# Window attention and a convolution on one core: split keys copied between partitions in place of a round trip through device memory

## Chip, core and metric

The program runs on one core of one Trainium2 chip. The metric is the time of one execution on the device in microseconds (us); of several runs the median is taken. The engines are TensorE (PE, matmuls; PEld is its weight loads), VectorE (DVE), ScalarE (ACT), GpSimd (POOL) and SyncE (SP), which here does nothing but issue transfers (DMAs) and wait.

## What is computed

Two residual steps on x of shape (2, 128, 128, 128), each behind a group norm with 32 groups. The first is attention in 8 by 8 windows with 16 heads of 8 channels, the second a 3 by 3 convolution. Cut to its core:

```
x = x + attention(group_norm(x))
x = x + conv3x3(group_norm(x)) + bias

attention(v):   g = clip((v * ac_w + ac_b) * v, 0, 6)
                q, k, v = qkv_w @ g, per window of 64 pixels and head of 8 channels
                o = softmax(q k^T / sqrt(8)) v
                return proj_w @ o + proj_b
```

## The kernel before, in words

For each of the 2 images there is an attention stage and then a convolution stage. The attention stage cuts the image into 32 units of 512 pixels (8 windows). It is a software pipeline written out by hand: each engine has a function `one` that is called once per iteration and issues its share of the work for units that lie up to 5 ahead and 3 behind. Order within an engine is the order of the code; between engines only semaphores order the work. `after(engine, s, unit)` waits until the event `s` of that unit has happened. Three buffers (`BUFS`) of each operand rotate.

The steps that the change and the prediction touch, for a unit d, with the lines of the kernel before:

- PE projects keys and queries into PSUM (`project`, L853 to L855). Each is split into a high half (fp16) and a low half (the rest, fp16), so that products keep their precision: ACT writes the high halves into the tile `qk` (keys L495, queries L503), DVE the low halves (queries L690, keys L692). `qk` has one buffer: parts 0 and 1 hold the low and high queries, 2 and 3 the high and low keys.
- The score matmuls want another layout: for a head the 8 channels times 3 halves (the "stack": high, low, high for keys; low, high, high for queries) must lie on 24 neighbouring partitions. [...]
- PE computes the scores of the unit twice: once plain (`scores`, L885) for the row maxima, which DVE takes (L654), and, an iteration later, transposed (`scores_t`, L899) with the maxima as two more rows of the stack, for ACT's exponentials (L448).
- The maxima of all heads are transposed by PE (L975), split by ACT (L499) and DVE (L686) into `m_pair`, and carried by SP into two rows of `q_bd` (`maxima`, L288, four transfers of 32 rows to one partition each).
- PE then multiplies with the values (`weigh`, L918, L926) and projects (L995).

SP goes through these transfers in a fixed order, one after the other: queries of a unit in, keys in, the maxima of the unit before it, the writes of the next unit, and so on. A wait at SP holds up all that stands behind it. ACT may overwrite the keys in `qk` (L495) once the write of the previous unit's keys has landed (`k_sent`), the queries (L503) once theirs has (`q_sent`).

The transposition L975 happens once per unit, so the time between two of them is the length of a unit.

Of the kernel before, what the change touches and what calls it, by code (L numbers as in the profile page):

```python
# [6 lines left out]
F16 = mybir.dt.float16  # L7
ALU = mybir.AluOpType
# [3 lines left out]
P = 128  # L12
# [10 lines left out]
UT = UW * WIN  # L23
# [3 lines left out]
HR, HG, HJ = 2, 4, 2  # L27
# [8 lines left out]
BUFS = 3  # L36
# [24 lines left out]
def build(nc, x, ac_w, ac_b, qkv_w, proj_w, proj_b, conv_w, conv_b, out):  # L61

    stackd = nc.dram_tensor("stack_scratch", [BUFS, 2, P, PARTS, UT], F16, kind="Internal").ap()

    ctx = ExitStack()
    with ctx:
# [73 lines left out]
        def sem(name, per=1):  # L140
            s = ctx.enter_context(nc.semaphore(name))
            names[name] = (s, per)
            return s
# [7 lines left out]
        v_out = sem("v_out", 4)  # L151
        q_sent = sem("q_sent", 32); k_sent = sem("k_sent", 32)
        q_in = sem("q_in", 64); k_in = sem("k_in", 32)
        s_done = sem("s_done", 4); max_done = sem("max_done", 4)
# [25 lines left out]
        def after(eng, s, unit, k=None):  # L180

            name = next(n for n, (h, _) in names.items() if h is s)
            per = names[name][1]
            eng.wait_ge(s, unit * per + (AHEAD * per + (per if k is None else k)))

        def pixels(u):

            return (u // ACROSS) * WS, (u % ACROSS) * UCOL

        block = ctx.enter_context(nc.Block())  # L190
# [52 lines left out]
        def _(sp):  # L243
# [13 lines left out]
            for b in range(BATCH):  # L257
                def write(which, d, md, lo, sent):
                    after(sp, lo, d)
                    to = stackd[md, which]  # L260
                    sp.dma_start(to[:, 0:2, :], qk[:, 2 * which:2 * which + 2, :]).then_inc(sent, 16)
                    sp.dma_start(to[:, 2, :], qk[:, 1 + which, :]).then_inc(sent, 16)

                def queries_in(d, md):
                    after(sp, q_sent, d)
                    after(sp, st_done, d - BUFS)
                    after(sp, q_in, d - 1)
                    q_rows = stackd[md, 0].rearrange("(r g j d) s t -> r j (d s) g t", r=HR, g=HG, j=HJ)
                    for r in range(HR):
                        for j in range(HJ):  # L270
                            at = 64 * r + HROWS * j
                            sp.dma_start(q_bd[at:at + HROWS, md, r, :, j, :], q_rows[r, j]).then_inc(q_in, 16)

                def keys_in(d, md):
                    after(sp, k_sent, d)
                    after(sp, st_done, d - BUFS)
                    after(sp, k_in, d - 1)
                    k_rows = stackd[md, 1].rearrange("(r g a) s t -> r (a s) g t", r=HR, g=HG)
                    for r in range(HR):
                        sp.dma_start(k_pl[64 * r:64 * r + ROWS, md, :, :], k_rows[r]).then_inc(k_in, 16)  # L280

# [9 lines left out]
                def one(i, m, live):  # L291
                    n = i + b * UNITS
                    if live(3):
                        queries_in(n + 3, (m + 3) % BUFS)
                        keys_in(n + 3, (m + 3) % BUFS)
                    if live(2):
                        maxima(n + 2, (m + 2) % BUFS)
                    if live(4):
                        after(sp, q_in, n + 1)
                        write(0, n + 4, (m + 4) % BUFS, q_lo_done, q_sent)  # L300
                        after(sp, k_in, n + 1)
                        write(1, n + 4, (m + 4) % BUFS, k_lo_done, k_sent)
                iterations(b, one)
# [119 lines left out]
        def _(act):  # L423
# [11 lines left out]
            act.wait_ge(pe_step, 3)  # L435
            a.copy(w_hi[:, :, :], ps[:, 0, 0:3 * P].rearrange("p (t d) -> p t d", t=3)).then_inc(act_step, 1)
            act.wait_ge(pe_step, 4)
            a.copy(pw[:, :], ps[:, 1, 0:P]).then_inc(act_step, 1)
            for b in range(BATCH):
# [25 lines left out]
                def one(i, m, live):  # L465
# [26 lines left out]
                    if live(3):  # L492
                        after(act, k_done, n + 3)
                        after(act, k_sent, n + 2)
                        a.copy(qk[:, 2, :], ps[:, GB, :]).then_inc(k_hi_done, 1)  # L495
# [59 lines left out]
        def _(dve):  # L555
# [41 lines left out]
            def weak_weights():  # L597

                for j in range(MATS // 4):
                    dve.wait_ge(act_step, 3 + j)  # L600
                    v.tensor_tensor(c_lo[:, 4 * j:4 * j + 4, :], ps[:, 2 + j, :].rearrange("p (t d) -> p t d", d=P),
                                    c_hi[:, 4 * j:4 * j + 4, :], ALU.subtract).then_inc(weights_done, 1)

            flat = img[:, :, :].rearrange("p r c -> p (r c)")
            for i in range(UNITS):
                if i == 2:
                    dve.wait_ge(act_step, 1)
                    link(v.tensor_tensor(w_lo[:, :, :], ps[:, 0, 0:3 * P].rearrange("p (t d) -> p t d", d=P), w_hi[:, :, :], ALU.subtract))
                dve.wait_ge(x_in[i * LOADS // UNITS], 16)
                stats = v.bn_stats(st[:, i, :], flat[:, i * UT:(i + 1) * UT])  # L610
# [208 lines left out]
        def _(pe):  # L819
# [36 lines left out]

            pe.wait_ge(act_step, 2)
            norm_mean(0)
# [188 lines left out]
```

## Time and profile before

| | us |
|---|---|
| median of 3 runs | 1202.87 |
| lowest, highest | 1198.44, 1207.99 |
| profiled execution, its own time | 1207.08 |
| its span, first to last instruction | 1205.3 |
| PE busy | 1015.8 (84% of the span) |
| DVE busy | 983.1 (82%) |
| ACT busy | 791.3 (66%) |
| mean granted TensorE clock | 0.947 of full speed |

The profile shows one execution. The first attention stage lies at about 40 to 470 us, the first convolution at 470 to 640, the second attention stage at 640 to 1060 and the second convolution behind it. SP has no busy time on the page, since issuing a transfer is not counted; the timeline of SP shows it: each row there is the issue of one or more transfers with the time that SP spent on it, not the transfer itself. "Landing" is the time from the start of an issue until its semaphore says that the data has arrived. "issue" as a releaser means that the profile shows nothing that the engine waited for, though a semaphore of a transfer may stand behind it.

### The profile page before, as it was taken

What the parts mean: (1) busy time and instruction counts of PE and PEld (TensorE: products, weight loads), DVE (VectorE), ACT (ScalarE), POOL (GpSimd) and SP (SyncE); (2) the same over time, 40 slices, a digit from 0 to 9 for tenths busy, and PEclk for the clock granted to TensorE, in tenths of its full rate; (3) what the DMA queues carried; (4) which work ended last, traced back from release to release, by engine and by line L of the source; (5) the groups of instructions that cost most, each with busy time, mean ns of one, the idle gap of its engine ahead of it and who ended that gap; (6) DMA issues with size and microseconds to landing.
All of it is one profiled execution on the core that took longest, in us unless ns stands there. A gap on an engine that the chain in (4) does not pass through costs nothing.

```text
span 1205.3 us, 52690 instructions
## 1 busy us (share of the span) xinstructions
PE 1015.8 (84%) x23011; PEld 582.6 (48%) x23011; DVE 983.1 (82%) x1312; ACT 791.3 (66%) x1327; POOL 503.8 (42%) x469
## 2 busy tenths in 40 slices
PE   0388999999999985998853899999999999779996
PEld 0155565556555652433321555556655655334442
DVE  6786888889888754899986788888988976379996
ACT  1257787778778774655532688878887877556663
POOL 5214454445444433233343245545454544404335
PEclk9879999999999997999986899999999999879998
DMA  8234444444444420133343454444444444001112
GB/s 307 84 118 125 136 138 138 136 137 128 135 142 135 142 64 1 44 129 108 105 157 122 123 150 139 136 137 138 144 132 148 134 142 126 4 1 53 70 70 88
DMA packets 114917, 140.59 MB, mean 117 GB/s; under 512 B 25088, under 2 KB 91008, under 8 KB 113664
## 3 DMA queue, kind: packets, MB, share of 16 engines
q1 hardware_dynamic: 114688, 137.23, 36.3%
q8 instruction: 182, 2.98, 1.1%
q14 instruction: 47, 0.39, 0.1%
HBM read 67.96 MB, written 67.11 MB: 112 GB/s over the span
## 4 chain that ended last, share of the span: by engine, by line
PE 63%; DVE 18%; issue 8%; DMA 4%; ACT 3%; SPq 2%; POOL 2%; POOLq 0%; DVEq 0%; ACTq 0%
PE ps L918 11%; PE ps L899 11%; PE ps L926 9%; PE ps L885 8%; PE ps L995 6%; PE ps L853 5%; DVE work L760 5%; PE ps L854 5%; PE ps L855 5%; DVE work L756 4%; PE ps L872 4%; DVE st L610 1%; SPq L288 1%; DVE work L738 1%; DMA q_bd<-stack_scratch 1%
## 5 line engine op out<-in xcount | busy, mean ns | idle before, releaser
L654 DVE TENSOR_REDUCE m_all<-ps 128x16 f32<-128x1024 f32 x256 | 313.5, 1225 | 114.9 <-PE ps L885 114.3
L370 POOL TENSOR_SCALAR work<-work 128x256 f32<-128x256 f32 x128 | 108.6, 849 | 401.2 <-DVE work L647 352.4
L885 PEld LDWEIGHTS ps<-k_pl,q_bd 48*64 48x64 f16 x8192 | 90.4, 111 | 174.5 <-issue 126.9
L448 ACT ACTIVATE late_probs<-ps,ws 128x1024 f32<-128x1024 f32 x128 | 142.8, 1116 | 44.6 <-PE ps L899 42.8
L853 PE MATMUL ps<-work,c_hi 128*128 128x512 f16 x384 | 148.3, 386 | 27.7 <-DVE work L760 27.7
L899 PE MATMUL ps<-q_bd,k_pl 128*64 128x256 f16 x2048 | 163.8, 282 | 7.5 <-ACT work L448 4.0
L885 PE MATMUL ps<-k_pl,q_bd 48*64 48x64 f16 x8192 | 118.6, 198 | 57.3 <-issue 39.4
L536 ACT CAST work<-work 128x512 f16<-128x512 f32 (+1 forms) x128 | 79.0, 622 | 115.8 <-DVE work L756 107.9
L448 ACT ACTIVATE work<-ps,ws 128x1024 f32<-128x1024 f32 x128 | 141.7, 1107 | 13.1 <-PE ps L899 11.5
L854 PE MATMUL ps<-work,c_lo 128*128 128x512 f16 x384 | 148.0, 385 | 0.0
L855 PE MATMUL ps<-work,c_hi 128*128 128x512 f16 x384 | 147.4, 384 | 0.0
L380 POOL TENSOR_TENSOR g_both<-work,g_both 128x512 f16<-128x512 f32 x64 | 99.9, 1561 | 54.4 <-ACT g_both L472 54.4
L899 PEld LDWEIGHTS ps<-q_bd,k_pl 128*64 128x64 f16 x2048 | 93.2, 110 | 58.7 <-issue 24.7
L647 DVE TENSOR_TENSOR work<-ps,work 128x512 f32<-128x512 f32 x128 | 87.3, 682 | 26.1 <-ACT work L457 26.1
L400 POOL TENSOR_TENSOR work<-work,img 128x512 f32<-128x512 f32 x30 | 48.1, 1603 | 139.3 <-DVE work L756 124.6
L760 DVE TENSOR_TENSOR work<-work 128x512 f16<-128x512 f32 (+1 forms) x128 | 101.7, 810 | 3.7 <-ACT work L536 3.1
L489 ACT COPY v_ext<-ps 64x256 f32<-64x256 f32 x256 | 93.3, 364 | 13.0 <-PE ps L872 8.1
L372 POOL TENSOR_TENSOR work<-work 128x256 f32<-128x256 f32 x128 | 93.2, 728 | 10.7
L455 ACT ACTIVATE work<-ps 128x256 f32<-128x256 f32 x128 | 49.2, 384 | 68.5 <-PE ps L926 68.5
L756 DVE TENSOR_TENSOR work<-g_both 128x512 f32<-128x512 f32 (+1 forms) x128 | 86.1, 693 | 4.8 <-ACT g_both L527 2.6
L918 PE MATMUL ps<-late_probs,v_ext 128*32 128x64 f32 x4096 | 87.6, 226 | 1.8 <-issue 1.6
L995 PE MATMUL ps<-work,pw 128*128 128x512 f32 x128 | 78.5, 698 | 7.0 <-POOL work L372 7.0
(126 smaller groups left out, 1894.1 us busy)
## 6 DMA issues: line engine op xcount, KB each, us to landing
stack_scratch<-work SPq DMA_DIRECT2D x128, 256.0 KB, 2.4
q_bd<-stack_scratch SPq DMA_DIRECT2D x256, 96.0 KB
k_pl<-stack_scratch SPq DMA_DIRECT2D x128, 192.0 KB, 3.5
stack_scratch<-work SPq DMA_DIRECT2D x128, 128.0 KB, 2.5
out_dram<-work SPq DMA_DIRECT2D x32, 512.0 KB, 2.9
img<-in_x_dram SPq DMA_DIRECT2D x8, 1024.0 KB, 13.4
img<-in_x_dram SPq DMA_DIRECT2D x16, 512.0 KB, 4.3
q_bd<-m_pair SPq DMA_DIRECT2D x256, 8.0 KB
```

The costliest lines, as they stand in the source:

```text
L370: g.tensor_scalar(near[h], near[h], -2.0, None, ALU.add).then_inc(less_done, 1)
L448: a.activation(probs[h][:, p % 2, :], ps[:, ST_B:ST_B + 2, :].rearrange("p w t -> p (w t)"), ACT.Exp, scale=ws[:, R_EXP:R_EXP + 1]).then_i ...
L654: v.tensor_reduce(m_all[:, 0, :, p], ps[:, S_B:S_B + 2, :].rearrange("p r (a k) -> p (r a) k", k=WIN), AX.X, ALU.max).then_inc(max_done, 1)
L756: v.tensor_tensor(plane[i][:, new_rows(t), :], column(t, l), column(t, r), op).then_inc(planes_done, 1)
L760: v.tensor_tensor(x_lo[:, i, ring_rows(t), :], plane[i][:, new_rows(t), :], x_hi[:, i, ring_rows(t), :], ALU.subtract).then_inc(x_lo_done, 1)
L853: t_.matmul(o, lhs_hi, rhs_hi, start=first, stop=False)
L854: t_.matmul(o, lhs_lo, rhs_hi, start=False, stop=False)
L855: return t_.matmul(o, lhs_hi, rhs_lo, start=False, stop=last)
L885: mm = t_.matmul(ps[64 * w:64 * w + 64, S_B + r, at:at + WIN], q_bd[rows, md, r, g, j, tok], k_pl[rows, md, g, tok], start=True, stop=True)
L899: mm = t_.matmul(ps[64 * c:64 * c + 64, ST_B + w, a * 256:a * 256 + 256], k_pl[:, md, g, tok], q_bd[:, md, :, g, :, tok], start=True, stop ...
L918: mm = t_.matmul(ps[32 * k:32 * k + 32, PV_B + h, at:at + WIN], v_ext[:, md, EACH * p + w, k, j:j + 2, :].rearrange("p s y -> p (s y)"), p ...
L995: t_.matmul(ps[:, GB, :], pw[:, :], o_n, start=True, stop=True).then_inc(proj_done, 1)
```

## The change

Queries keep their way through device memory. The keys no longer take it: each of the three parts of the stack is copied straight from the tile `qk` to its rows of `k_pl`, in six transfers (three parts, two halves of the partitions). A transfer takes 64 neighbouring partitions of one part and puts them on 16 partitions, every third one, four pieces of 512 elements on each. For that to come out right the channels of the key projection are laid out in another order, which is done once, when the weights are turned: the copies of the weights, one instruction each on ACT and DVE before, are three, and the one for the keys permutes columns. The scratch loses its half for the keys. ACT's write of the high keys (L495 before, L502 now) waits for `k_in` of the unit before instead of `k_sent`. The order of SP's transfers is written out anew: maxima, queries out, keys across, queries in.

```diff
-    stackd = nc.dram_tensor("stack_scratch", [BUFS, 2, P, PARTS, UT], F16, kind="Internal").ap()
+    stackd = nc.dram_tensor("stack_scratch", [BUFS, P, PARTS, UT], F16, kind="Internal").ap()
...
-        q_in = sem("q_in", 64); k_in = sem("k_in", 32)
+        q_in = sem("q_in", 64); k_in = sem("k_in", 16 * HR * PARTS)
...
+        def by_head(k):
+
+            cols = ps[:, 0, k * P:k * P + P]
+            return cols.rearrange("p (r g j d) -> p r j d g", r=HR, g=HG, j=HJ) if k == 1 else cols
+
+        def by_column(w, k):
+
+            return w[:, k, :].rearrange("p (r j d g) -> p r j d g", r=HR, j=HJ, g=HG) if k == 1 else w[:, k, :]
...
-                def write(which, d, md, lo, sent):
-                    after(sp, lo, d)
-                    to = stackd[md, which]
-                    sp.dma_start(to[:, 0:2, :], qk[:, 2 * which:2 * which + 2, :]).then_inc(sent, 16)
-                    sp.dma_start(to[:, 2, :], qk[:, 1 + which, :]).then_inc(sent, 16)
+                def write_queries(d, md):
+                    after(sp, q_lo_done, d)
+                    sp.dma_start(stackd[md, :, 0:2, :], qk[:, 0:2, :]).then_inc(q_sent, 16)
+                    sp.dma_start(stackd[md, :, 2, :], qk[:, 1, :]).then_inc(q_sent, 16)
...
                 def keys_in(d, md):
-                    after(sp, k_sent, d)
+                    after(sp, k_lo_done, d)
                     after(sp, st_done, d - BUFS)
                     after(sp, k_in, d - 1)
-                    k_rows = stackd[md, 1].rearrange("(r g a) s t -> r (a s) g t", r=HR, g=HG)
-                    for r in range(HR):
-                        sp.dma_start(k_pl[64 * r:64 * r + ROWS, md, :, :], k_rows[r]).then_inc(k_in, 16)
+                    for s, part in enumerate((2, 3, 2)):
+                        for r in range(HR):
+                            sp.dma_start(k_pl[64 * r + s:64 * r + ROWS:PARTS, md, :, :], qk[64 * r:64 * r + 64, part, :]).then_inc(k_in, 16)
...
                     n = i + b * UNITS
+                    if live(1):
+                        maxima(n + 1, (m + 1) % BUFS)
                     if live(3):
+                        after(sp, q_in, n)
+                        write_queries(n + 3, (m + 3) % BUFS)
+                        keys_in(n + 3, (m + 3) % BUFS)
                         queries_in(n + 3, (m + 3) % BUFS)
-                        keys_in(n + 3, (m + 3) % BUFS)
-                    if live(2):
-                        maxima(n + 2, (m + 2) % BUFS)
-                    if live(4):
-                        after(sp, q_in, n + 1)
-                        write(0, n + 4, (m + 4) % BUFS, q_lo_done, q_sent)
-                        after(sp, k_in, n + 1)
-                        write(1, n + 4, (m + 4) % BUFS, k_lo_done, k_sent)
...
-            a.copy(w_hi[:, :, :], ps[:, 0, 0:3 * P].rearrange("p (t d) -> p t d", t=3)).then_inc(act_step, 1)
+            for k in range(3):
+                a.copy(by_column(w_hi, k), by_head(k)).then_inc(act_step, 1)
...
                         after(act, k_done, n + 3)
-                        after(act, k_sent, n + 2)
+                        after(act, k_in, n + 2)
                         a.copy(qk[:, 2, :], ps[:, GB, :]).then_inc(k_hi_done, 1)
...
-                    link(v.tensor_tensor(w_lo[:, :, :], ps[:, 0, 0:3 * P].rearrange("p (t d) -> p t d", d=P), w_hi[:, :, :], ALU.subtract))
+                    for k in range(3):
+                        link(v.tensor_tensor(by_column(w_lo, k), by_head(k), by_column(w_hi, k), ALU.subtract))
```

SP's queue, one unit in the middle of an attention stage, before (the semaphores that an issue waits for stand in brackets; `x3` is three more of the same):

```order
L288 DMA q_bd<-m_pair 1x32x128 [waits st_done,m_lo_done]
L288 DMA q_bd<-m_pair 1x32x128 x3
L261 DMA stack_scratch<-work 128x1024 [waits q_lo_done,q_in]
L262 DMA stack_scratch<-work 128x512
L261 DMA stack_scratch<-work 128x1024 [waits k_lo_done,k_in]
L262 DMA stack_scratch<-work 128x512
L272 DMA q_bd<-stack_scratch 24x4x512 [waits q_in,st_done,q_sent]
L272 DMA q_bd<-stack_scratch 24x4x512 x3
L280 DMA k_pl<-stack_scratch 48x4x512 [waits k_in,st_done,k_sent]
L280 DMA k_pl<-stack_scratch 48x4x512
```

The same unit in the changed kernel (`work` is the memory in which the tile `qk` lies):

```order
L297 DMA q_bd<-m_pair 1x32x128 [waits st_done,m_lo_done]
L297 DMA q_bd<-m_pair 1x32x128 x3
L269 DMA stack_scratch<-work 128x1024 [waits q_lo_done,q_in]
L270 DMA stack_scratch<-work 128x512
L289 DMA k_pl<-work 16x4x512 [waits k_in,st_done,k_lo_done]
L289 DMA k_pl<-work 16x4x512 x5
L280 DMA q_bd<-stack_scratch 24x4x512 [waits q_in,st_done,q_sent]
L280 DMA q_bd<-stack_scratch 24x4x512 x3
```

Between the queries' way out and their way back there were two transfers, and behind them two more; now there are six between and none behind: 14 issues per unit before, 16 now. The wait for `k_sent` is gone, and the last transfer to be issued for a unit is now one of the queries, not one of the keys.

ACT's queue at the split of the keys, before:

```order
L448 ACTIVATE work<-ps,ws 128x1024 [waits pv_done,st_done]
L495 CAST work<-ps 128x512 [waits k_sent,k_done]
L499 ACTIVATE m_pair<-ps 64x128 [waits m_in,mt_done]
L503 CAST work<-ps 128x512 [waits q_sent,q_done]
L448 ACTIVATE late_probs<-ps,ws 128x1024 [waits pv_done,st_done]
```

And in the changed kernel:

```order
L455 ACTIVATE work<-ps,ws 128x1024 [waits pv_done,st_done]
L502 CAST work<-ps 128x512 [waits k_in,k_done]
L506 ACTIVATE m_pair<-ps 64x128 [waits m_in,mt_done]
L510 CAST work<-ps 128x512 [waits q_sent,q_done]
L455 ACTIVATE late_probs<-ps,ws 128x1024 [waits pv_done,st_done]
```

The order is the same; the cast of the keys now waits for the arrival of the last unit's keys at their rows (`k_in`), and the split of the maxima stands behind it. PE's and POOL's queues are unchanged.

## Rows read from the trace of the kernel before

**Rows 1.** Windows, L975 alone: stretch, its length, busy time with count, clock, DMA.

```profile
104.80:432.30 327.50, 7.36 (x27) 3.66 (x26) 0.98 0.46 136
698.20:1019.30 321.10, 7.36 (x27) 3.67 (x27) 0.99 0.48 141
```

**Rows 2.** Timeline of PE, three units' L975 and one wait: start, us, line, what, [idle before].

```profile
214.46 0.27 PE L975 MATMUL ps<-ident,m_all 128*128 128x128 f32 x1
...
225.60 0.27 PE L975 MATMUL ps<-ident,m_all 128*128 128x128 f32 x1
...
229.85 0.23 PE L885 MATMUL ps<-k_pl,q_bd 48*64 48x64 f16 x5 [1.97 <-issue]
...
240.26 0.27 PE L975 MATMUL ps<-ident,m_all 128*128 128x128 f32 x1
```

**Rows 3.** The chain that ended last, 289 to 304 us: start, us, what.

```profile
289.39 0.29 DVE m_pair L686
...
289.70 0.51 SPq L288
...
297.36 1.69 SPq L272
...
299.09 3.77 DMA q_bd<-stack_scratch
...
304.06 0.45 PE ps L885 x32
```

**Rows 4.** Timeline of SP, one unit: start, us of issuing, line, count.

```profile
264.26 3.39 SPq L288 DMA_DIRECT2D q_bd<-m_pair  x4
267.74 0.53 SPq L261 DMA_DIRECT2D stack_scratch<-work  x1
268.31 0.43 SPq L262 DMA_DIRECT2D stack_scratch<-work  x1
268.84 0.39 SPq L261 DMA_DIRECT2D stack_scratch<-work  x1
269.28 0.46 SPq L262 DMA_DIRECT2D stack_scratch<-work  x1
270.38 1.57 SPq L272 DMA_DIRECT2D q_bd<-stack_scratch  x4
272.05 0.99 SPq L280 DMA_DIRECT2D k_pl<-stack_scratch  x2
```

**Rows 5.** Single lines of SP: ns per issue, min/median/max; landing (of L280) in us.

```profile
L288 SPq DMA_DIRECT2D q_bd<-m_pair x256: 502/591/1989, 68.2 to 1033.9; - x128
L272 SPq DMA_DIRECT2D q_bd<-stack_scratch x256: 290/375/1888, 51.7 to 1016.3; - x128
L246 SPq DMA_DIRECT2D work<-in_L_conv_proj_w_dram x2: 696/726/755, 1.3 to 2.1; - x2
L280 SPq DMA_DIRECT2D k_pl<-stack_scratch x128: 307/308/1762, 53.4 to 1017.1; - x128
...
DMA to landing us min/median/max: 2.8/3.5/4.6
```

**Rows 6.** SP's own waits, 104.81 to 432.35 us: total, times, longest.

```profile
SPq L288 <- DVE m_pair L686: 63.1, 27, 6.1
SPq L272 <- DMA stack_scratch<-work: 23.4, 27, 2.6
```

**Rows 7.** Timeline of ACT and PE at the split of keys and maxima.

```profile
288.62 0.58 ACT L495 CAST work<-ps 128x512 f16<-128x512 f32 x1
...
288.74 0.27 PE L975 MATMUL ps<-ident,m_all 128*128 128x128 f32 x1
...
289.09 0.27 ACT L499 ACTIVATE m_pair<-ps 64x128 f16<-64x128 f32 x1
```

**Rows 8.** The page, DMA issues: count and KB of each.

```profile
q_bd<-m_pair SPq DMA_DIRECT2D x256, 8.0 KB
```

**Rows 9.** Timeline of DVE while x is loaded.

```profile
16.16 0.56 DVE L608 TENSOR_TENSOR w_lo<-ps,w_hi 128x384 f16<-128x384 f32 x1
```

More of the change, by code:

```diff
@@ L151, in build @@
         v_out = sem("v_out", 4)
-        q_sent = sem("q_sent", 32); k_sent = sem("k_sent", 32)
-        q_in = sem("q_in", 64); k_in = sem("k_in", 32)
+        q_sent = sem("q_sent", 32)
+        q_in = sem("q_in", 64); k_in = sem("k_in", 16 * HR * PARTS)
         s_done = sem("s_done", 4); max_done = sem("max_done", 4)
@@ L267, in queries_in @@
                     after(sp, q_in, d - 1)
-                    q_rows = stackd[md, 0].rearrange("(r g j d) s t -> r j (d s) g t", r=HR, g=HG, j=HJ)
+                    q_rows = stackd[md].rearrange("(r g j d) s t -> r j (d s) g t", r=HR, g=HG, j=HJ)
                     for r in range(HR):
@@ L599, in weak_weights @@
                 for j in range(MATS // 4):
-                    dve.wait_ge(act_step, 3 + j)
+                    dve.wait_ge(act_step, 5 + j)
                     v.tensor_tensor(c_lo[:, 4 * j:4 * j + 4, :], ps[:, 2 + j, :].rearrange("p (t d) -> p t d", d=P),
@@ L606, in _ @@
                 if i == 2:
-                    dve.wait_ge(act_step, 1)
-                    link(v.tensor_tensor(w_lo[:, :, :], ps[:, 0, 0:3 * P].rearrange("p (t d) -> p t d", d=P), w_hi[:, :, :], ALU.subtract))
+                    dve.wait_ge(act_step, 3)
+                    for k in range(3):
+                        link(v.tensor_tensor(by_column(w_lo, k), by_head(k), by_column(w_hi, k), ALU.subtract))
                 dve.wait_ge(x_in[i * LOADS // UNITS], 16)
@@ L855, in three @@
                 return t_.matmul(o, lhs_hi, rhs_lo, start=False, stop=last)
-            pe.wait_ge(act_step, 2)
+            pe.wait_ge(act_step, 4)
             norm_mean(0)
```

## The prediction, made before the changed kernel was run

> **What bounds the kernel now.** I read the windows first, with the transposition L975 alone, because it comes once per unit and so gives the length of a unit. In the full part of the two attention stages 27 units take 327.5 and 321.1 us, 12.13 and 11.89 us each [rows 1]. Next I looked in PE's timeline for the shortest unit: from 214.46 to 225.60 it takes 11.14 us, with PE going from one matmul to the next [rows 2]. The unit behind it takes 14.66 us: PE stands for 1.97 us before the scores L885, and the other 1.55 us lie in slower matmuls after that wait. So PE sets a floor of 11.14 us, and what stands above it, 27 x (0.99 + 0.75) = 47 us in both stages, is waiting and what follows from it. That is the most that a change of transfers can win there.
>
> The chain of waits tells what PE waits for [rows 3]: the split of the maxima (L686), the issue of their transfers at SP (L288), the writes to the scratch, the reads of the queries (L272), and the scores. The keys (L280) are issued behind the queries and land last, though the chain names the queries. From L975 at 288.74 [rows 7] to the scores at 304.06 it is 15.32 us. PE wants the operands 2.28 us after the next L975 (229.85 less 1.97, from 225.60) [rows 2], which leaves 11.14 + 2.28 = 13.42 us. A chain that is longer makes PE wait by the difference. The chain is as long as SP's issues make it, and these vary: an L272 that has a median of 0.375 us takes 1.69 us in this chain [rows 3, 5].
>
> The unit in rows 4 is a quick one. L288 starts 0.96 us after L975, as in rows 3 and 7; the first write follows 3.48 us later; the second L280 starts at about 272.40 and, with the median landing of 3.5 us [rows 5], its keys are there at 275.90, 8.16 us after the first write. The chain is 0.96 + 3.48 + 8.16 = 12.60 us: no wait. So chains lie on both sides of the 13.42 us, and the sign of the change depends on a few tenths of a microsecond at SP.
>
> **The change, part by part.** *Removed*, per unit: two issues that write keys (0.39 and 0.46 us), two that read them (about 0.31 and 0.45 us) [rows 4], and SP's wait for `k_sent`. *Added*: six issues across partitions, of p us each with 0.04 us between. They stand between the queries' write and their read, where SP waited 23.4 / 27 = 0.87 us for the write to land [rows 6]; that wait is their only cover. The keys need no round trip any more and land before the queries do, so the chain now ends with the last L272.
>
> New chain from the first write: 1.10 us to the third issue (268.84 less 267.74), 6 x (p + 0.04), 0.10 us gap, 1.19 us to the start of the last L272 (1.57 less 0.38) [rows 4, 5], and its landing. The landing of L272 is not shown; it is bounded by the 2.8 us that L280, with twice the bytes, needed at least [rows 5], and the 3.77 us of a slow moment [rows 3]. I take 2.8. That makes 5.19 + 6 x (p + 0.04), to be set against 8.16 us; it breaks even at p = 0.455 us.
>
> No row shows such an issue. Transfers whose two sides have the same shape cost little: L272 0.375, L280 0.31 to 0.45 [rows 4, 5]. Two lines have sides that fold differently, as the new ones do (64 rows on one side, 16 rows of four pieces on the other): L288 (32 rows to one) with 0.59 us and L246 with 0.73 us [rows 5]. I take L288's 0.59, since it too goes between partitions; the ends are 0.31 and 0.73. With 0.59 the new chain is 8.97 us, 0.81 us longer than the old. The ends give -0.87 and +1.65 us, and 0.375 gives -0.48.
>
> *What that is worth.* A wait of PE also puts off the next L975, which gives the transfers already under way that much more time, so a unit grows by only half of what the chain grows: with chain C the unit settles at (C + 11.14 - 2.28) / 2. Half of 0.81 is 0.40 us, over the 54 full units 22 us. The end at 0.31 gives -23 us, that at 0.73 +45 us.
>
> *SP itself.* It now waits 63.1 + 23.4 us in 27 units, 3.20 us each [rows 6], so it works 8.93 us per unit. Less 1.9 for the four issues removed and their gaps, plus 6 x 0.63, it works 10.8 us: still below 11.14, but a slow issue no longer finds slack.
>
> *Start.* The weights' three copies and three subtractions in place of one each: DVE's L608 takes 0.56 us between statistics that run without a gap [rows 9]; three pieces with a wait behind each I put at 1.0 us, so +0.4 us. ACT's copies lie before that and nothing is behind them but `pw`.
>
> **Sum.** 1207.1 (the profiled execution's own time) + 22 + 0.4 = 1229.5 us. The median of the runs stands 4.2 us lower than that execution, so 1225 us.
>
> **Rivals.**
>
> *A, faster: the issues are cheap.* Price 0.31 to 0.375 us, as for the other transfers of SP; it decides below 0.455 us, at SP between the queries' write and read. Then the keys drop out of the end of the chain: a chain shorter by 0.48 to 0.87 us, -13 to -23 us, 1190 to 1180 us, say 1185. For it: every transfer with sides of one shape has this price, whatever its size. Against: both lines with unequal sides are dearer, also L288 with only 8 KB in a transfer [rows 8].
>
> *B, no change: the wait moves to ACT.* ACT may cast the next keys (L495, now L502) only when the last ones have arrived, and the split of the maxima stands behind it. That closes a loop of one unit: 0.47 us from the cast to L499 and 0.30 to L686 [rows 3, 7], 0.31 to L288, 2.5 for its four issues, 1.10 for the two writes, 5 x 0.63 to the last key issue, 2.8 landing: 10.6 us. SP's slow issues add: 8.93 us of work per unit against about 7.0 when all are quick [rows 4, 5] is 1.9 us, some 1.4 of it in these twelve issues. 12.0 us per unit is what it takes today, so 1203 us, with ACT's wait in place of PE's. It decides above about p = 0.41. Where it comes on top of the longer chain, the time goes beyond 1229.
>
> *C: issuing hardly counts.* If only landings counted, the queries would start back 2.64 us after the first write as now (270.38) and land 1.19 + 2.8 us later: 6.63 us, 1.53 less, half of it over 54 units 41 us, 1161 us. The Trainium skill has this rule in "DMA: Bandwidth & Descriptors", section "Issuing engines are not separate DMA queues": the sequencer's time to initiate a transfer is usually small relative to the transfer itself. The trace does not bear it out here: four issues of 8 KB hold SP for 3.39 us [rows 4, 8], and L272's wait is ended by a landing in only 0.87 us of 12.
>
> **Chances.** A measurement of this kernel tells about 1% (12 us) from no change. Forecast (unequal sides are dear, the chain gets longer, slower by more than 1%) 0.45; B, with prices around 0.455, within 1%, 0.25; A 0.25; C 0.05. So faster 0.30, same 0.25, slower 0.45. The range goes from A with the cheapest price, 1180, to the dearest price, 1207.1 + 45 + 0.4 - 4.2 = 1248, rounded up to 1250. C and what is beyond 1250 make up less than 2 in 10. The forecast's own range is 1215 to 1250.
>
> **What would show it.** SP's row of the six issues decides: at or above 0.5 us each the forecast stands, below 0.45 rival A does. L975 should come every 12.3 to 12.6 us; PE's waits before L885 should be more frequent, the chain should run over the queries' read, and SP's wait for `q_sent` should be gone. If ACT's cast of the keys has idle time ended by the keys' transfer, B is at work. If the issues are dear and the time still falls, the step from chain to unit length is wrong. If the landing of the queries' read changes by more than half a microsecond, because less is carried beside it, the 2.8 us was the mistake.

## The result and the profile after

The changed kernel takes 1228.61 us in the median of 4 runs (1225.96 to 1233.07), beside 1201.18 us for the kernel before in the same rounds: a ratio of 1.0223, 95% interval [1.0166, 1.0281]. It is slower, as forecast (1225 us). The profiled execution took 1226.23 us, with a span of 1224.5 us, 19.2 us more than the span of before. (The medians differ by 27.4 us, since the profiled execution of before, 1207.08 us, was one of its longer ones.)

The windows first, with the transposition (now L983) alone, as in [rows 1]:

```profile
102.60:435.50 332.90, 7.40 (x28) 3.72 (x27) 0.98 0.32 102
705.90:1040.80 334.90, 7.38 (x28) 3.72 (x27) 0.97 0.32 101
```

27 units now take 332.9 and 334.9 us, 12.33 and 12.40 us each, 5.4 and 13.8 us more than before. That is the whole 19.2 us; what lies around these stretches adds up to nothing. PE is busy for as long as before (1017.4 us in all, 1015.8 before), so nearly all of it is idle time of PE. The last two columns show that less is moved (32% against 46 and 48% of the DMA engines' time, 101 GB/s against 136 and 141): the change does save traffic, and it does not help.

PE's timeline, a unit with a wait, as in [rows 2]:

```profile
213.37 0.27 PE L983 MATMUL ps<-ident,m_all 128*128 128x128 f32 x1
...
218.16 0.64 PE L893 MATMUL ps<-k_pl,q_bd 48*64 48x64 f16 x32 [2.52 <-DMA q_bd<-stack_scratch]
...
229.84 0.27 PE L983 MATMUL ps<-ident,m_all 128*128 128x128 f32 x1
```

The floor has not moved: a quick unit still takes 11.14 us. But of the 62 distances between transpositions within the two stages only 13 are below 11.35 us, where 23 were before. PE waits here by name for the queries' read. The page's rows of the score matmuls, before and after (behind the second bar: PE's idle time ahead of them, and what ended most of it):

```profile
L885 PE MATMUL ps<-k_pl,q_bd 48*64 48x64 f16 x8192 | 118.6, 198 | 57.3 <-issue 39.4
```

```profile
L893 PE MATMUL ps<-k_pl,q_bd 48*64 48x64 f16 x8192 | 118.3, 199 | 73.2 <-DMA q_bd<-stack_scratch 57.4
```

The waits of the whole execution (total us, times, longest):

```profile
PEld ps L893 <- DMA q_bd<-stack_scratch: 83.4, 53, 5.5
...
PE ps L893 <- DMA q_bd<-stack_scratch: 57.4, 46, 5.0
...
DVE m_pair L694 <- ACT m_pair L506: 44.4, 42, 2.4
...
ACT work L502 <- DMA k_pl<-work: 37.6, 31, 3.4
```

Two things are new. PE's waits have grown by 16 us and end with another operand: before, 34 of its 47 waits ahead of the scores (40.7 us) ended as the keys landed, by the times of the landings in the trace, though the profile books most of them as "issue"; now 46 of 58 (57.4 us) end with the queries. And ACT's cast of the keys, whose wait for a transfer came to 1.2 us in all before, waits 37.6 us for the keys' arrival, with the split of the maxima behind it. Both lie in one chain, which is the chain that ended last, 198 to 218 us (start, us, what), answering to [rows 3]:

```profile
198.50 0.59 SPq L289
199.14 3.31 DMA k_pl<-work
...
203.01 0.28 ACT m_pair L506
203.31 0.29 DVE m_pair L694
203.62 0.55 SPq L297
...
206.17 1.11 SPq L269
207.32 0.43 SPq L270
...
207.86 0.59 SPq L289
...
212.77 0.49 SPq L280
...
214.17 3.95 DMA q_bd<-stack_scratch
...
218.16 0.64 PE ps L893 x20
```

Read it from the top: the last key issue of one unit, its landing, ACT, DVE, the maxima's issues, the two writes, six key issues from 207.86 to 212.66 (one of them a slow one of 1.62 us), the queries' four, their landing, PE. The page's chain gives SP's issues 28% of the span, L289 alone 13%. ACT's timeline at the same place, as in [rows 7], shows the cast let go by the keys:

```profile
202.53 0.58 ACT L502 CAST work<-ps 128x512 f16<-128x512 f32 x1 [1.72 <-DMA k_pl<-work]
203.01 0.27 ACT L506 ACTIVATE m_pair<-ps 64x128 f16<-64x128 f32 x1
```

SP's timeline of a unit, as in [rows 4], and the single lines (ns min/median/max), as in [rows 5]:

```profile
215.79 2.45 SPq L297 DMA_DIRECT2D q_bd<-m_pair  x4
218.34 0.53 SPq L269 DMA_DIRECT2D stack_scratch<-work  x1
218.91 0.43 SPq L270 DMA_DIRECT2D stack_scratch<-work  x1
219.86 4.54 SPq L289 DMA_DIRECT2D k_pl<-work  x6
224.51 1.77 SPq L280 DMA_DIRECT2D q_bd<-stack_scratch  x4
```

```profile
L289 SPq DMA_DIRECT2D k_pl<-work x384: 545/594/2144, 50.5 to 1039.6; - x192
```

```profile
L280 SPq DMA_DIRECT2D q_bd<-stack_scratch x256: 291/383/1727, 54.5 to 1041.7; - x128
```

The price of a key issue is 0.594 us in the median, as L288's 0.591 was [rows 5]. The six together take 4.72 us in the mean, since some issues are slow. The other lines kept their prices.

### The profile page after: what moved, and what is told of

It is laid out like the page before. It is cut to its first block, busy times and chain, and to the rows that moved or that the text cites. A ratio compares the mean times of both kernels' runs of the same rounds, so it can differ in the third digit from the quotient of the medians.

```text
span 1224.5 us, 52757 instructions
## 1 busy us (share of the span) xinstructions
PE 1017.4 (83%) x23011; PEld 582.0 (48%) x23011; DVE 981.7 (80%) x1314; ACT 791.0 (65%) x1329; POOL 503.7 (41%) x469
## 4 chain that ended last, share of the span: by engine, by line
SPq 28%; PE 26%; DVE 20%; DMA 10%; issue 9%; ACT 4%; POOL 2%; POOLq 0%; ACTq 0%; DVEq 0%
SPq L289 13%; SPq L297 8%; DVE work L768 5%; DMA q_bd<-stack_scratch 5%; DVE work L764 4%; PE ps L926 4%; PE ps L907 4%; DMA k_pl<-work 4%; PE ps L1003 3%; PE ps L893 3%; SPq L280 3%; PE ps L934 3%; PE ps L861 3%; PE ps L862 2%; PE ps L863 2%
## 5 line engine op out<-in xcount | busy, mean ns | idle before, releaser
L893 PE MATMUL ps<-k_pl,q_bd 48*64 48x64 f16 x8192 | 118.3, 199 | 73.2 <-DMA q_bd<-stack_scratch 57.4
L455 ACT ACTIVATE work<-ps,ws 128x1024 f32<-128x1024 f32 x128 | 141.5, 1106 | 12.9 <-PE ps L907 11.2
```

The source lines that it names most:

```text
L455: a.activation(probs[h][:, p % 2, :], ps[:, ST_B:ST_B + 2, :].rearrange("p w t -> p (w t)"), ACT.Exp, scale=ws[:, R_EXP:R_EXP + 1]).then_i ...
L893: mm = t_.matmul(ps[64 * w:64 * w + 64, S_B + r, at:at + WIN], q_bd[rows, md, r, g, j, tok], k_pl[rows, md, g, tok], start=True, stop=True)
```

## The experiments

Theory: the six issues at SP between the queries' write and their read make the chain longer. Rivals: the price itself is owed to something avoidable (unequal folding, both sides on the chip, few rows), the wait of ACT is the loss and not the longer chain, the transfers' bytes and landings are, or SP's issuing as a whole, in whatever order, sets the pace.

### Is it the folding, the bytes or the source that makes an issue dear?

**equal_sides** (leaves out the keys' own layout):

```diff
- sp.dma_start(k_pl[64 * r + s:64 * r + ROWS:PARTS, md, :, :], qk[64 * r:64 * r + 64, part, :])
+ sp.dma_start(k_pl[64 * r:64 * r + 64, md, s, :], qk[64 * r:64 * r + 64, part, :])
```

> The changed kernel, but each of the six key transfers puts its 64 rows of 512 elements on 64 rows of k_pl (one column block per part) instead of 16 rows of four pieces: the same source, the same 64 KB, the same number of issues, and both sides have one shape. The keys then lie in the wrong rows; only the time is of use. Theory 1 (a transfer whose sides fold differently costs SP 0.59 us to issue, and that price lengthens the chain): the six issues fall from a median of 0.594 us to 0.38 to 0.46, the six together from 4.70 us on average to about 3.5, the queries land about 1 us earlier after the first write (10.6 us on average now), and the time falls to 1195 to 1208 us. Theory 2 (copying between partitions is slow in itself, in the transfer and its landing): the issue stays near 0.59 us, or falls and the time stays at 1222 to 1232.

**quarter_bytes** (128 of the 512 columns; leaves out the rest of the keys):

```diff
+ sp.dma_start(k_pl[64 * r + s:64 * r + ROWS:PARTS, md, :, 0:128], qk[64 * r:64 * r + 64, part, 0:128])
```

> The changed kernel, but each key transfer carries only the first 128 of 512 elements of every row: the same six issues of 64 rows to 16, a quarter of the bytes. Three quarters of the keys are left out. Theory 1 (the issue is what counts): issues stay at 0.59 us, time 1218 to 1232 us, since only the landing (2.15 us after the last issue at the median) can get some tenths shorter. Theory 2 (the transfers themselves load the DMA engines and land late): the time falls below 1212 us.

**from_memory** (the source is a tensor of zeros in device memory, `zerosd`; leaves out the keys):

```diff
+ sp.dma_start(k_pl[64 * r + s:64 * r + ROWS:PARTS, md, :, :], zerosd[64 * r:64 * r + 64, s, :])
```

> The changed kernel, but the six key transfers read their 64 rows of 512 elements from a scratch in device memory that holds zeros (filled once at the start) and put them on the same 16 rows of four pieces as before: same destination, count and size; the source is no longer a tile on the core. The keys are left out (zeros). With sides of one shape the issue had stayed at 0.597 us, so the folding is not what makes it dear. Theory 1a (an issue is dear when both ends lie in on-chip memory): the issue falls to 0.35 to 0.46 us, the queries land about 1 us earlier after the first write, and the time falls to 1198 to 1212 us. Theory 1b (the price comes from the 64 rows or from the destination): the issue stays at 0.59 us and the time at 1220 to 1234 us.

**rows_128** and **pieces_128** (both leave out the keys' own layout):

```diff
+ sp.dma_start(k_pl[:, md, s, 256 * r:256 * r + 256], qk[:, part, 256 * r:256 * r + 256])
```

```diff
+ j, t = 2 * (s % 2), 256 * (s // 2)
+ sp.dma_start(k_pl[64 * r:64 * r + 64, md, j:j + 2, t:t + 256],
+              qk[64 * r:64 * r + 64, part, :].rearrange("p (a t) -> p a t", a=2))
```

> Six key transfers of the same 64 KB, but each from 128 rows of 256 elements to 128 rows of 256 elements, in place of 64 rows of 512 (leaves out: the keys' own layout, so the scores are of other operands). If the price of an issue goes with how few rows a transfer has: about 0.43 us as for the other transfers with 128 rows, the six together 2.8 us in place of 4.70, the queries' landing some 1.9 us earlier, and 1195 to 1210 us. If the price comes from what stands before the issue (the sixth of a row of issues at one queue, or transfers still under way), it stays near 0.59 us, and the time near 1228. If issuing is not the loss at all, the price falls and the time stays near 1228.

> Six key transfers of the same 64 KB from 64 rows to 64 rows as in equal_sides, but each row in two pieces of 256 elements (leaves out: the keys' own layout). If the price goes with the number of pieces: about 0.43 us and 1195 to 1210 us, like rows_128. If it goes with the number of rows: 0.59 us and about 1228. If rows_128 stays at 0.59 too, so must this one.

The key issues of the five in this order (ns min/median/max):

```profile
L289 SPq DMA_DIRECT2D k_pl<-work x384: 462/597/1957, 50.1 to 1040.0; - x192
```

```profile
L289 SPq DMA_DIRECT2D k_pl<-work x384: 546/594/2221, 50.7 to 1041.8; - x192
```

```profile
L293 SPq DMA_DIRECT2D k_pl<-zeros_scratch x384: 537/594/2256, 50.6 to 1037.2; - x192
```

```profile
L289 SPq DMA_DIRECT2D k_pl<-work x384: 464/602/2152, 50.5 to 1037.0; - x192
```

```profile
L290 SPq DMA_DIRECT2D k_pl<-work x384: 591/613/2147, 50.3 to 1038.4; - x192
```

| | us, median | ratio to before, 95% |
|---|---|---|
| equal_sides | 1227.41 | 1.0208 [1.0154, 1.0261] |
| quarter_bytes | 1218.82 | 1.0150 [1.0079, 1.0221] |
| from_memory | 1227.82 | 1.0205 [1.0150, 1.0261] |
| rows_128 | 1227.07 | 1.0203 [1.0161, 1.0244] |
| pieces_128 | 1239.37 | 1.0322 [1.0263, 1.0382] |

None of it moves the median price by more than 0.02 us: equal sides, a quarter of the bytes, a source in device memory, twice the rows, twice the pieces, always 0.59 to 0.61 us. Each theory of what makes it dear (the folding, the source, the number of rows or pieces) missed. The same queue issues the queries' read at 0.38 us in the same unit, so there is something that makes an issue dear; what it is stays open. What stands ahead of an issue has a part in it (medians by place, from the single issues in the traces): in the changed kernel the first key issue of a unit costs 0.591 us and the five behind it 0.594, but in equal_sides the first costs 0.511 and the five behind it 0.597; and the first of the queries' four reads costs 0.489 us right behind the keys, where it cost 0.316 behind a wait in the kernel before. No run was made to vary this alone.

With the price the time stays too, in equal_sides, from_memory and rows_128. A quarter of the bytes changes it by less than the intervals tell apart (the median is 10 us lower; the profiled execution, 1232.27 us, was its longest), so bytes can be a part of the loss, but not the whole. pieces_128 is slower in the median; but its profiled execution took 1226.97 us, as the others did, and the three that took 1238.69 to 1248.59 us have no trace. ACT's wait for the keys in that trace (51.4 us, 38 times, against 37.6) does not explain them: from_memory has 54.1 us of it at 1226.12 us. Why they were longer stays open.

### How much of the loss is ACT's wait?

**two_buffers**: the high keys get a second buffer (a piece of `work` that is free in this stage), so ACT waits for the keys of two units back. Nothing is left out.

```diff
+        k_hi = [qk[:, 2, :], part(6144, 256).bitcast(F16)]
...
-                        after(act, k_in, n + 2)
-                        a.copy(qk[:, 2, :], ps[:, GB, :]).then_inc(k_hi_done, 1)
+                        after(act, k_in, n + 1)
+                        a.copy(k_hi[(n + 3) % 2], ps[:, GB, :]).then_inc(k_hi_done, 1)
...
+                        after(dve, k_in, n + 2)
...
```

> The changed kernel with a second buffer for the high keys: ACT's cast of the keys waits for the arrival of the keys two units back, not one, and the wait for the last unit's keys moves to DVE's low keys, which stand behind the split of the maxima. In the changed kernel ACT's cast waits 37.6 us for key transfers and the first maxima issue starts 1.65 us after L975 on average against 0.96 us in a quick unit. Theory 1 (issues lengthen the queries' chain, and ACT's wait adds to it): the chain gets about 0.7 us shorter, half of that over 54 units is 19 us, time 1205 to 1214 us, with PE's waits for the queries still there. Theory 3 (rival B of the prediction: ACT's wait is the whole loss): all of it comes back, 1195 to 1203 us. Theory 4 (ACT's wait only follows from a late chain and costs nothing of its own): 1222 to 1232 us.

**four_buffers**: the low keys get one too, so that DVE's write of them waits two units back as well (`after(dve, k_in, n + 1)`).

> The kernel with a second buffer for the high keys, and now one for the low keys as well, so that DVE's low keys wait for the arrival of the keys two units back too. With the high keys alone the wait had moved to DVE: 62 us before the low keys, 45 times. Theory 1 (waits for the keys' arrival cost beside the queries' chain): a few us less than that kernel's 1214.7, 1204 to 1212 us. Rival (DVE's wait is slack): 1212 to 1218 us.

(The 62 us of DVE's wait that this expectation starts from are those of split_two, below; in two_buffers it is 4.4 us, as its rows below show.)

Two_buffers: 1214.71 us, ratio 1.0132 [1.0054, 1.0210]. Four_buffers: 1213.01 us, 1.0080 [1.0046, 1.0115], clear of the changed kernel's interval. Windows and waits of two_buffers:

```profile
104.85:429.50 324.65, 7.38 (x28) 3.71 (x27) 1.00 0.33 105
700.30:1023.05 322.75, 7.38 (x28) 3.72 (x27) 0.99 0.33 104
```

```profile
PE ps L895 <- DMA q_bd<-stack_scratch: 50.3, 41, 5.1
...
DVE work L702 <- DMA k_pl<-work: 4.4, 8, 1.2
```

ACT's wait is gone, and with it 0.9 points of the 2.2% in two_buffers, whose interval still overlaps that of the changed kernel, and 1.4 in four_buffers. The two runs cannot be told apart. PE waits for the queries' read nearly as often as in the changed kernel (41 times against 46). So the wait for the keys' arrival was roughly half of the loss; what is left, 0.8 to 1.3%, goes with the six issues, be it through the chain to the queries or through SP's work as a whole: these two runs do not separate them.

### The order of the issues

**split_two**: two_buffers, and only three of the key issues stand before the queries' read, the other three behind it.

```diff
...
+                        keys_in(n + 3, (m + 3) % BUFS, pieces[:3])
                         queries_in(n + 3, (m + 3) % BUFS)
+                        keys_in(n + 3, (m + 3) % BUFS, pieces[3:])
```

> The kernel with the second buffer, and another order at SP: three key transfers, the queries' four reads, then the other three key transfers. SP issues the same 16 transfers per unit. Theory 1 (what counts is how late the last operand lands, not how many issues SP has): the three first keys just cover the landing of the queries' write (2.4 us at least), the queries land about 1.4 us earlier after the first write than the 8.6 us of a quick unit, the last keys about 8.2 us after it, so the chain ends 0.4 us earlier than with the second buffer alone: 10 us less than that kernel, 1195 to 1205 us. Rival (SP's issuing as such, some 10.8 us of a unit of 12.3, sets the pace, so the order does not matter): the same time as with the second buffer alone, within 5 us.

**split_four**: the same on four_buffers.

> Both kinds of keys with two buffers, and the order three keys, queries, three keys at SP. With only the high keys doubled this order gave 1205.4 us, 1.0045 times the kernel before. Theory 1 (late keys hold DVE there, since the last keys are issued behind the queries): 1192 to 1202 us, as fast as the kernel before or a little faster. Rival (nothing but the chain to the last landing counts, which stays as it is): 1202 to 1208 us.

Split_two took 1205.39 us, ratio 1.0045 [1.0012, 1.0077]; split_four 1208.65 us, 1.0057 [1.0022, 1.0091]. The waits of split_two:

```profile
DVE work L704 <- DMA k_pl<-work: 62.0, 45, 3.1
...
PE ps L897 <- DMA q_bd<-stack_scratch: 4.9, 4, 2.0
```

PE hardly waits for the queries' read any more: three issues fewer stood before it. But it waits for the keys instead, which are the last to land again: its idle time ahead of the scores is 62.5 us, where it was 66.8 in two_buffers, and 40 of its 49 waits (50.1 us) end as the keys land. DVE waits for the late keys too; in split_four it no longer does, and the time is no better. The medians are 9.3 and 4.4 us below those of the same buffers in the plain order, and in both pairs the intervals overlap. Of the 10.2 us between the profiled spans of two_buffers and split_two (1209.9 and 1199.7), 8.2 are PE's busy time (1014.7 and 1006.5, at a granted clock of 0.947 and 0.952), not waits. So the order of the issues counts for little here, and these runs neither prove the chain nor rule out SP's work as a whole. No order of six issues came out below the kernel before.

### The issues on another engine

**keys_pool**: GpSimd issues the six key transfers, behind the residual addition and ahead of the quotient in its order.

```diff
+                    after(pool, k_lo_done, d)
...
+                            g.dma_start(k_pl[64 * r + s:64 * r + ROWS:PARTS, md, :, :], qk[64 * r:64 * r + 64, part, :]).then_inc(k_in, 16)
...
+                    if live(3):
+                        keys_in(n + 3, (m + 3) % BUFS)
                     if live(-1):
                         quotient(n - 1, 0)
```

> The changed kernel with its six key transfers issued from GpSimd's queue, behind the residual addition, so that SP issues ten transfers per unit and goes from the queries' write straight to the wait for its landing. Theory 1 (SP's issues between the queries' write and read are the loss): the queries land 6.5 to 8 us after the first write instead of 10.6, and if GpSimd (42% busy) can issue six transfers in under 6 us per unit, PE's waits all but go: a floor of 11.14 us per unit, 1150 to 1175 us. If an issue costs GpSimd over 1 us, GpSimd and the keys' arrival become the bound: 1190 to 1260 us. Rival (the loss lies in the copies between partitions themselves, whoever issues them): 1215 to 1235 us.

1718.02 us, ratio 1.4256 [1.4189, 1.4322]: neither theory had this. POOL's timeline, then DVE's and PE's at the same place:

```profile
312.10 3.07 POOL L373 DMA_DIRECT2D k_pl<-work  x6 [11.77 <-issue]
315.19 0.86 POOL L379 TENSOR_SCALAR work<-work 128x256 f32<-128x256 f32 x1
```

```profile
310.04 0.68 DVE L705 TENSOR_TENSOR work<-ps,work 128x512 f16<-128x512 f32 x1
```

```profile
318.62 2.05 PE L1008 MATMUL ps<-work,pw 128*128 128x512 f32 x2 [6.51 <-POOL work L381]
```

The 11.77 us ahead of the transfers are booked as "issue", but they are mostly a wait: the first transfer waits for the low keys of its unit (`k_lo_done`), which DVE writes until 310.72 us (L705), while POOL's last work of its own ended at 300.33 us. Of the 11.77 us 10.4 lie before DVE is done. The six issues themselves show as 3.07 us, 0.51 us each, not more than SP's. Behind them in POOL's order stands the quotient (L379, L381); PE's projection waits for it (6.51 us here, 380.6 us in 58 times in the whole execution) before PE comes to the next unit's keys, and for these POOL waits next. So the place that the transfers got in POOL's order closes a ring, 20.48 us long per unit. The run says nothing of the theory, and it shows no dear issue from GpSimd; the same transfers behind the quotient were not tried.

### Fewer issues

**three_in_four**: each channel gets four rows of the stack in place of three. The fourth holds zeros, or the maxima in two of the rows. All 128 partitions of a part then go to every fourth row of `k_pl` in one transfer of 128 KB. Nothing is left out.

```diff
+SLOTS = 4
-ROWS = HJ * HD * PARTS
-HROWS = HD * PARTS
+ROWS = HJ * HD * SLOTS
+HROWS = HD * SLOTS
...
-                        for r in range(HR):
-                            sp.dma_start(k_pl[64 * r + s:64 * r + ROWS:PARTS, md, :, :], qk[64 * r:64 * r + 64, part, :]).then_inc(k_in, 16)
+                        sp.dma_start(k_pl[s:P:SLOTS, md, :, :], qk[:, part, :]).then_inc(k_in, 16)
...
-                            at = 64 * r + ROWS + k
+                            at = 64 * r + SLOTS * k + PARTS
```

The scratch for the queries has four parts too, the fourth zeroed once at the start.

> Three key transfers in place of six: every head channel gets four rows in the stack in place of three (the fourth holds zeros or the maxima), so that all 128 partitions of a part go to every fourth row of k_pl in one transfer of 128 KB; the queries' read carries four rows in place of three (128 KB in place of 96 KB) in its four transfers. If the issues at SP between the queries' write and their read are the loss: three issues at 0.43 to 0.60 us take 1.4 to 1.9 us in place of 4.70, the queries land about 2.8 to 3.3 us earlier after the first write, that is at 7.3 to 7.8 us plus what the larger read costs, SP has 14 - 1 issues per unit, fewer than the kernel before, and ACT's wait for the keys nearly goes: units of 11.3 to 11.8 us, 1180 to 1203 us. If a transfer's issue costs by its bytes or pieces, the three cost 1.2 us each and it stays near 1228. If landings are the loss (a third more bytes for queries, keys in larger transfers), it stays at 1215 to 1235 although the issues take less.

**six_in_four**: three_in_four with each key transfer cut in two halves of the columns. Nothing is left out.

```diff
+                        for c in range(2):
+                            sp.dma_start(k_pl[s:P:SLOTS, md, :, 256 * c:256 * c + 256],
+                                         qk[:, part, 256 * c:256 * c + 256]).then_inc(k_in, 16)
```

> three_in_four with its key transfers cut in two halves of the columns: six issues of 64 KB in place of three of 128 KB, all else the same, bytes and rows too. If the number of issues is what counts: six at 0.59 us as before, 4.5 us together in place of 2.3, the queries land about 2.2 us later than in three_in_four, units of 12.4 to 12.6 us, 1225 to 1245 us. If the four rows per channel (another layout of the rows, fewer waits of PE for another reason) made it faster: 1160 to 1180 us with six issues too. Between 1180 and 1225 both would have a part.

Three_in_four: **1164.01 us** (1163.20 to 1166.51, 4 runs), ratio 0.9674 [0.9638, 0.9711], 3.3% faster than the kernel before. Six_in_four: 1246.83 us, 1.0384 [1.0312, 1.0456]. Windows of the two, three_in_four first:

```profile
99.30:406.85 307.55, 7.37 (x28) 3.70 (x27) 1.00 0.40 123
669.45:974.15 304.70, 7.40 (x28) 3.73 (x27) 1.00 0.40 123
```

```profile
103.95:447.42 343.47, 7.37 (x28) 3.70 (x27) 0.98 0.37 109
715.45:1055.28 339.83, 7.40 (x28) 3.73 (x27) 0.98 0.37 110
```

Their key issues in the same order:

```profile
L292 SPq DMA_DIRECT2D k_pl<-work x192: 536/602/2134, 50.6 to 971.6; - x192
```

```profile
L293 SPq DMA_DIRECT2D k_pl<-work x384: 529/602/2292, 49.9 to 1053.8; - x192
```

Rows, bytes and layout are the same; an issue costs 0.602 us whether it carries 128 or 64 KB. Three more of them per unit make the unit 1.33 and 1.30 us longer (12.72 and 12.59 against 11.39 and 11.29). The pieces are half as long in six_in_four, which by itself is worth nothing that can be seen (rows_128 against the changed kernel: 1227.07 and 1228.61 us), or little beside the 83 us between these two (pieces_128, with pieces of that length too, is 11 us slower in the median). With the changed kernel's number of issues the fourth row costs 18 us (1246.83 against 1228.61). Against the changed kernel three_in_four has pieces of the same length, the same bytes of keys and a third more of queries, and half the key issues: 64.6 us less, and less than the 1180 to 1203 us that were expected. SP's timeline of three_in_four, and PE's waits, with the page's row:

```profile
217.43 0.53 SPq L273 DMA_DIRECT2D stack_scratch<-work  x1
218.00 0.43 SPq L274 DMA_DIRECT2D stack_scratch<-work  x1
218.54 2.81 SPq L292 DMA_DIRECT2D k_pl<-work  x3
221.46 1.97 SPq L284 DMA_DIRECT2D q_bd<-stack_scratch  x4
```

```profile
PE ps L896 <- DMA q_bd<-stack_scratch: 12.3, 14, 3.3
```

```profile
L896 PE MATMUL ps<-k_pl,q_bd 64*64 64x64 f16 x8192 | 117.2, 197 | 29.0 <-DVE m_all L665 15.4
```

The last query's issue is over 6.0 us after the first write started (223.43 less 217.43); in the changed kernel's unit above it was 7.9 us (226.28 less 218.34). PE's idle time ahead of the scores is 29.0 us, half of the 57.3 of the kernel before; it waits 14 times for the queries, and 42 of 62 distances are below 11.35 us: the kernel stands at PE's floor for most units. So between these kernels the number of key issues at SP decides the time; how much of that goes through the chain to the queries, how much through ACT's wait and how much through SP's work as a whole is told apart only roughly.

## Why the prediction was right, and where its reasons were not

**The price of a key issue: right as a number, wrong as a reason.** 0.59 us was taken and 0.594 measured. The reason given, that the sides fold differently, is refuted by equal_sides (0.597). That sides of one shape make an issue cheap did not hold in the rows at hand either: the writes, 128 rows on both sides, cost 0.39 to 0.53 us [rows 4]. The row chosen for its folding has the same price for a reason that stays open, so the number was luck.

**The chain behind the first write: right in sign, too large.** As a mean over the 54 full units of both stages, worked out from the trace's issues and semaphores, the last operand lands 10.68 us after the first write (the queries), where it was 10.19 us (the keys): 0.49 us more, not 0.81. The step that was off is the comparison: a reckoned chain of 8.97 us was set against the 8.16 us of one quick unit. On average the old chain is 2.03 us longer than that unit's, and the new one only 1.71 us longer than reckoned. The shortest is 9.25 us (8.49 before). The landing of the read takes 2.63 us in the median, 2.2 at least, where 2.8 was taken; before it took 2.92, so that sign of a mistake did not come. The wait for the write (0.87 us a unit) is indeed gone.

**The chain ahead of the first write: the step that was missing.** The sum had nothing there. Measured over the same units, the first write comes 4.47 us after the transposition, where it was 3.93. That is rival B's mechanism, ACT's cast held by the keys, which the prediction treated as an alternative and in one sentence as something that could come on top. It came on top: 0.54 us of the 1.03 us of both, and two_buffers and four_buffers give back a like share of the loss (about 40 and 65%). The time did not go beyond 1229 for it, as that sentence said it would, because the other part was smaller by 0.32 us. That 1225 us came so near was in part luck: one term was too large and one was missing.

**From chain to unit: right.** Half of 1.03 us is 0.5 us a unit; measured 0.20 and 0.51 in the two stages, 0.36 in the mean, and 19.2 us in the span where 22 was forecast. From the changed kernel to six_in_four the chain grows by 0.76 us and the unit by 0.29. To three_in_four it shrinks by 1.96 us and the unit by 1.03, nearly down to the floor. So the rule holds roughly; as an absolute value it is 0.3 to 0.5 us low, perhaps since a mean over units hides that a quick one cannot fall below 11.14 us.

**SP's work.** 10.8 us per unit were forecast. SP's wait for the maxima in the first stretch is now

```profile
SPq L297 <- DVE m_pair L694: 31.4, 24, 4.5
```

that is 1.16 us in a unit of 12.33, so SP works 11.2 us: PE's floor is reached by SP too, and little slack is left for a slow issue.

**The start.** DVE's three subtractions take 0.95 us in place of 0.56 [rows 9], the first transposition starts at 67.8 us in place of 67.1. The sum had 0.4 us there; the 0.3 us more count for nothing beside the rest.

**The rivals.** A fell by the price, 0.594 against 0.455. B was at work, as a part. C fell: issuing counts. The Trainium skill ("DMA: Bandwidth & Descriptors", section "Issuing engines are not separate DMA queues") says that initiating a transfer is usually small beside it. For a single transfer that holds here (the queries' read: 0.38 us of issue, 2.63 us to its landing); in this loop it does not make issues free: in six_in_four the bytes of three_in_four go in three more issues a unit, and the time is 83 us longer. The Trainium skill's "Perfetto Trace Analysis", section "What "DMA-bound" means", names a second case, an issuing engine whose track is solid with DMA issues, and says that large descriptors matter there. Its first half nearly fits SP here (11.2 of 12.33 us); the second does not: pieces of a quarter of the size left the price at 0.594 us, and it was the number of issues that brought the time down.

## What to carry to other kernels

Where one queue issues all transfers of a loop, count its issues by their measured price before counting bytes: a copy that skips a round trip through memory loses if it needs more issues, and wins if the layout lets it go in fewer. When a buffer's release is moved to a later event, look at who writes that buffer next and what stands behind the writer on its engine; here that was worth about as much as the longer chain itself. The same holds for a transfer that is given to another engine: in keys_pool its wait held up work on which the next unit's keys depended. Between two rows with different prices, the likeness that seems to explain the price should be tried and not believed.

## What was not expected of the hardware

- An issue of these key transfers costs SP 0.59 to 0.61 us in the median, whatever it carries (16 to 128 KB, 64 or 128 rows, one or two pieces, from the chip or from memory), while the queries' read costs 0.38 us on the same queue. What sets it was not found; what stands ahead of an issue has a part (0.489 against 0.316 us for the same read).
- In the changed kernel 127 of SP's 1088 issues took over 0.9 us (1.34 in the median), 97 us more in all than at 0.59 us each. Every one of the 127 overlaps in time a packet of the instruction queue (182 packets in the execution); of the other 961 issues 154 do. (In the kernel before it is 105 of 106.) The two are seen together; no run varied it.
- Six transfers issued from GpSimd show as 3.07 us on that engine. The idle time ahead of them, booked as "issue", was mostly a wait for a semaphore.
